# Handing over PSUM banks and halves one by one in a four-stage recurrent and attention network, with clock-keeping products in the last attention unit

## The chip, the cores and the metric

The kernel runs on one core of a Trainium2 chip. The metric is device time in microseconds (us) for one execution, from inputs in device memory to the output in device memory; lower is better. The engines are named as in the profile: PE is TensorE's matmul stream, PEld its weight loads, DVE is VectorE, ACT is ScalarE, POOL is GpSimd, SP issues DMAs. PSUM is the memory that TensorE writes; here it is used as eight banks of 512 float32 columns on 128 partitions.

## The reference

Sixteen sequences of 128 tokens with 256 channels pass through four layers, all in float32:

- a recurrent layer: layer norm, token shift (difference to the token before), five low-rank mixings of the shifted input, then projections of the mixed inputs to decay, key, value, receptance and gate; a recurrence `s = w * s + k v` with a state of 8 x 8 for each of 32 heads, read out by `r`; a norm over each head, the gate, an output projection and a residual; then a channel mix (layer norm, shift, `sigmoid(r) * (relu(k)^2 @ Wv)`) and a residual
- cross-attention to a context of 128 tokens with 16 heads of 16 channels, whose output goes through a projection and a scalar gate
- a second recurrent layer with other weights
- cross-attention with biases, followed by a layer norm and an MLP of 1024 hidden channels with GELU.

## The kernel before

The sequences are worked on in four groups of four (`G` = 4, `NB` = 4, `T` = 128 tokens, `C` = 256 channels in `HALF` = 2 halves of 128). Each group meets two mixers (one for each recurrent layer) and two attention units, so there are eight of each, in the order of `STEPS`. Three generator programs are interleaved on each engine:

- `head` (letter H): the first half of a mixer. Layer norm into `z`, transposed by TensorE into `PA`, copied to `XN`; `SX` is the shift; `mix` makes the first mixed input in `X5`; a low-rank product gives `low` and `thT`. Then for f = 0 to 4: `maa(f)` multiplies into both banks of `PA` (L990), `mix_low_rank` turns it into a mixed input in two passes over the two halves (L400, then L408), and a projection follows from `X5` into `PA` (L1022 and L1028 for the decay, L1046 for key, value and receptance, L1061 for the gate). `turn` (L417) transposes `PA` into the layout of the recurrence.
- `recurrence` (R): outer products `A_` (L425), scans (L498), products with `R_` (L506), and the sum over the state on TensorE (L1073), then norm, gate, output projection into `PB` (L1093) and the addition to `X`.
- `attn` (A): the channel mix (L576, L389, L954, L967, L586, L587), then the attention in 16 jobs of four heads each, its output projection (L967), and in layer 1 the MLP (L1255, L1264).

On every engine the strings of `ORDER` say which program advances to its next `yield`; each engine executes in that order and nothing overtakes. Engines meet through semaphores that are counted: `COUNTS` says how often each is raised in a unit. Before the change nearly all of them are raised once for a whole two-bank tile:

```python
for h in range(HALF):
    last = v.tensor_tensor(blocks(X5[use % 2][:])[:, h], split(pa4(h)), split(XN[:, h, :, 1:T + 1]), ALU.add)
last.then_inc(sem["r_mixed"], 1)
```

`keep_clock(o, n)` (L975) issues n products of the identity with itself that nobody reads; in `head` it is called through `fill`, for the first mixer only. A float32 product of 256 or 512 columns appears in the trace as two matmul records.

## Time and profile before

| | |
|---|---|
| Time, median of three runs | 1308.97 us (1307.58 to 1309.52) |
| The profiled execution | 1307.29 us, of which the trace's span is 1305.5 us |
| PE busy | 1127.7 us, 86% of the span |
| DVE busy | 859.1 us, 66% |
| ACT busy | 490.2 us, 38% |
| Mean granted TensorE clock | 0.923 of 2.4 GHz |

An engine's busy time is the sum of its instructions. A granted clock of 1.00 in a stretch means 2.4 GHz throughout, 0.50 means 1.2 GHz throughout. The chain that ended last is 63% PE and 26% DVE.

### The profile page before, as it was taken

What the parts mean: (1) busy time and instruction counts of PE and PEld (TensorE: products, weight loads), DVE (VectorE), ACT (ScalarE), POOL (GpSimd) and SP (SyncE); (2) the same over time, 40 slices, a digit from 0 to 9 for tenths busy, and PEclk for the clock granted to TensorE, in tenths of its full rate; (3) what the DMA queues carried; (4) which work ended last, traced back from release to release, by engine and by line L of the source; (5) the groups of instructions that cost most, each with busy time, mean ns of one, the idle gap of its engine ahead of it and who ended that gap; (6) DMA issues with size and microseconds to landing.
All of it is one profiled execution on the core that took longest, in us unless ns stands there. A gap on an engine that the chain in (4) does not pass through costs nothing.

```text
span 1305.5 us, 13985 instructions
## 1 busy us (share of the span) xinstructions
PE 1127.7 (86%) x5302; PEld 754.2 (58%) x5302; DVE 859.1 (66%) x1060; ACT 490.2 (38%) x1502; POOL 115.5 (9%) x92
## 2 busy tenths in 40 slices
PE   6856889898998898889798989989899898987868
PEld 4634557565756575647555756546656476564645
DVE  4597599769985997599755695446965459642320
ACT  1002215722572267215732732425332355221731
POOL 1021010101010100021000111000010001100000
PEclk9987889988998899979998989979999899997869
DMA  9000000000000000000000000000000000000000
GB/s 371 22 0 1 0 17 13 1 1 17 13 1 2 16 13 1 1 16 13 2 17 9 5 1 1 33 8 5 1 1 33 6 7 1 0 17 2 12 1 17
DMA packets 13317, 22.63 MB, mean 17 GB/s; under 512 B 3777, under 2 KB 10561, under 8 KB 12610
## 3 DMA queue, kind: packets, MB, share of 16 engines
...
## 4 chain that ended last, share of the span: by engine, by line
PE 63%; DVE 26%; ACT 5%; issue 4%; POOL 1%; DMA 1%; SPq 0%; POOLq 0%; DVEq 0%; ACTq 0%
PE QA L967 7%; PE PA L1046 6%; PE PB L1073 5%; DVE S_ L498 5%; PE QA L1264 4%; PE PA L990 4%; PE QB L1183 3%; PE QA L1159 3%; DVE A L506 3%; PE QB L954 2%; ACT big L889 2%; PE QA L1199 2%; DVE A L425 2%; PE QB L1112 2%; PE QB L1186 2%
## 5 line engine op out<-in xcount | busy, mean ns | idle before, releaser
L889 ACT ACTIVATE big<-QB,nmax 128x128 f32<-128x128 f32 x512 | 181.2, 375 | 72.8 <-DVE nmax L614 72.6
L498 DVE TENSOR_TENSOR_SCAN S_<-W_,A 128x1024 f32<-128x1024 f32 x64 | 154.3, 2432 | 0.2
L1073 PE MATMUL PB<-A,common_w 128*128 128x256 f32 x512 | 133.1, 405 | 23.0 <-DVE A L506 22.9
L614 DVE TENSOR_REDUCE nmax<-QB 128x4 f32<-128x512 f32 x128 | 86.7, 684 | 68.4 <-PE QB L1183 41.0
L1073 PEld LDWEIGHTS PB<-A,common_w 128*128 128x128 f32 x512 | 99.9, 204 | 49.9 <-DVE A L506 28.8
L1046 PE MATMUL PA<-rwkv_w,X 128*128 128x256 f32 x384 | 105.3, 426 | 11.6 <-DVE X L408 11.5
L889 ACT ACTIVATION_READ_ACCUMULATOR big<-QB,nmax 128x1 f32 x512 | 110.3, 215 | 0.0
L1183 PE MATMUL QB<-big,QX 128*128 128x256 f32 x384 | 101.2, 387 | 0.0
L1199 PE MATMUL QA<-common_w,big 128*128 128x128 f32 x512 | 83.1, 287 | 19.7 <-ACT XT L898 12.6
L1046 PEld LDWEIGHTS PA<-rwkv_w,X 128*128 128x128 f32 x384 | 79.2, 213 | 32.1 <-DVE X L408 17.2
L1199 PEld LDWEIGHTS QA<-common_w,big 128*128 128x128 f32 x512 | 63.0, 146 | 47.6 <-ACT big L889 22.0
L1183 PEld LDWEIGHTS QB<-big,QX 128*128 128x128 f32 x384 | 75.2, 196 | 13.3 <-issue 2.3
L400 DVE SCALAR_TENSOR_TENSOR PA<-PA,rwkv_w,SX 128x512 f32<-128x512 f32 x80 | 56.6, 752 | 39.9 <-PE PA L990 39.7
L990 PE MATMUL PA<-low,rwkv_w 32*128 32x512 f32 x128 | 64.0, 619 | 13.7 <-DVE K_ L417 8.5
L700 POOL TENSOR_SCALAR aveps<-amv 128x4 f32<-128x4 f32 x20 | 11.6, 578 | 707.8 <-DVE amv L373 707.8
L506 DVE TENSOR_TENSOR A<-R_,S_ 128x2048 f32<-128x2048 f32 x32 | 73.1, 2284 | 0.6
L425 DVE TENSOR_TENSOR A<-K_,V_ 128x2032 f32<-128x2032 f32 x32 | 72.6, 2267 | 1.3 <-PE PB L1073 0.7
L1177 PE MATMUL QB<-mrow,first_row 128*128 128x512 bf16 x128 | 50.4, 394 | 16.9 <-ACT big L889 16.0
L1264 PE MATMUL QA<-mlp_w,big 128*128 128x256 f32 x256 | 59.2, 384 | 0.8 <-ACT big L933 0.8
L898 ACT ACTIVATE XT<-QA 128x512 f32<-128x512 f32 x64 | 38.7, 605 | 40.1 <-PE QA L1199 40.0
L1264 PEld LDWEIGHTS QA<-mlp_w,big 128*128 128x128 f32 x256 | 47.6, 190 | 10.2 <-ACT big L933 1.6
L408 DVE TENSOR_TENSOR X<-PA,XN 128x512 f32<-128x512 f32 x80 | 51.4, 684 | 1.2
...
## 6 DMA issues: line engine op xcount, KB each, us to landing
rwkv_w<-in_rwkv_w SPq DMA_DIRECT2D x2, 2674.0 KB, 13.6
...
```

The source lines that it names most:

```text
L425: return v.tensor_tensor(A_[c % 2][:, :, :, 1:T], K_[:, :, 0:T - 1].unsqueeze(1).broadcast_to([P, DC, RS, T - 1]), V_[:, DC * c:DC * c + D ...
L498: last = v.tensor_tensor_scan(S_[:, d].rearrange("p k t -> p (k t)"), W_[:].rearrange("p k t -> p (k t)"), A_[c % 2][:, d].rearrange("p k ...
L506: v.tensor_tensor(A_[c % 2][:], R_[:].unsqueeze(1).broadcast_to([P, DC, RS, T]), S_[:], ALU.mult)\
L614: v.tensor_reduce(nmax[:, n % 2], bank(2 + n % 2).rearrange("p (j s) -> p j s", j=JH), AX.X, ALU.max, negate=True).then_inc(sem["a_max"], 1)
L889: last = s.activation(PR[:, n % 2, j], bank(2 + n % 2)[:, j * T:(j + 1) * T], ACT.Exp, bias=nmax[:, n % 2, j:j + 1], accum_out=den[:, b, h ...
L967: last = t.matmul(o, lhs(h, b), w[:, h], start=(h == 0), stop=(h == HALF - 1 and bias is None))
L990: last = t.matmul(pa(h), w2, tt, start=True, stop=True, tile_position=(rows, 0))
L1046: last = t.matmul(PA[:, a * C:(a + 1) * C], src[:, h, a * P:(a + 1) * P], wt[:, h], start=(h == 0), stop=(h == HALF - 1))
L1073: last = t.matmul(y, ident, A_[c % 2][:, :, k], start=(c % 2 == 0 and k == 0), stop=False, skip_group_check=True)
L1183: last = t.matmul(o, QX[b % 2][:, i, h], K2[:, :, h, b * T:(b + 1) * T], start=False, stop=True, skip_group_check=True)
L1199: last = t.transpose(bank(0)[:, j * T:(j + 1) * T], PR[:, n % 2, j], ident)
L1264: t.matmul(o, H_[:, m, b * T:(b + 1) * T], proj[:, m], start=(m == 0), stop=False)
```

## The change

- Hand-overs in halves. Nearly every semaphore that was raised once for a tile of two banks (or two halves) is raised once for each, and the consumer waits for the half that it needs. `mix`, `mix_low_rank` and `maa` signal each half; the subtraction of the token shift (`shift`) is issued for each half; `turn` is two transposes, one for each bank of `PA`, with a `yield` between; the additions to `X`, the square and centring in the norm of the recurrence, `tanh`, `relu` and square in ScalarE, the final addition and the store are in two parts.
- TensorE's token projections go by pairs: for two output blocks of 256 columns in one bank, first the products of channel half 0, then those of half 1 (`token_pair`). Number and size of the products stay the same.
- In the recurrence, the product that adds `V_` to `PB` goes before the last chunk rather than after it. The squares `SQ` are stored so that their sum reads neighbouring elements. `z` lives in `X5[0]` and not in `SX`.
- The first half of attention's output projection waits for `a_rb` and the first `a_on` only.
- Clock-keeping products: fewer in the first mixer (57 instead of 83), and new ones in the last attention unit (16, 2, 24, 3, 24 and 4 of them, 73 in all), written to `PA`.
- All four strings of `ORDER` are new. In VectorE's, the two outer products of the first mixer's recurrence (`RR`) now stand together right behind the turn of `V_`, with the mixing of f = 3 behind both; before, the mixing stood between them.

```diff
     "VectorE":
-        "HHAHHHHHHHHHHHRHHRHHHRRRRHRRRHRRRRHRRRRHHRRRHRHRRRHHHRAHAHHAAHRRHHAAHAHHRRRARARRRAAHRARARARARARAAHRR"
...
+        "HHAHHHHHHHHHHHHHHRRHHHHHHRRRRHRRRHRRHRRHRHRRRHHRRHRHRRRHHRHRRAHAHHAAHHRRHHAAAHHAHRRARARHRRARARRRAARH"
...
-        z = SX[:].rearrange("p h b t -> p (h b t)").rearrange("p (b c) -> p b c", b=NB)
         X5 = [sb(f"X5_{i}", [HALF, NB, T]) for i in range(2)]
+        z = X5[0][:].rearrange("p h b t -> p (h b t)").rearrange("p (b c) -> p b c", b=NB)
...
-        SQ = A_[1][:, 0]
+        SQ = A_[1][:, 0].rearrange("p k t -> p (k t)").rearrange("p (t d) -> p t d", d=RS)
...
-                        sp.wait_ge(sem["a_out"], u.at("a_out", 1))
-                        sp.dma_start(out[u.group], result).then_inc(sem["st_out"], 16)
-                sp.wait_ge(sem["st_out"], 16 * G)
+                        for k in range(2):
+                            sp.wait_ge(sem["a_out"], u.at("a_out", k + 1))
+                            sp.dma_start(out[u.group][:, 2 * k:2 * k + 2], result[:, 2 * k:2 * k + 2]).then_inc(sem["st_out"], 16)
+                sp.wait_ge(sem["st_out"], 32 * G)
...
                     for h in range(HALF):
-                        last = v.scalar_tensor_tensor(dst[:, h], sx[:, h], vec[:, h:h + 1], xn[:, h, :, 1:T + 1],
-                                                      ALU.mult, ALU.add)
-                    last.then_inc(done, 1)
+                        v.scalar_tensor_tensor(dst[:, h], sx[:, h], vec[:, h:h + 1], xn[:, h, :, 1:T + 1],
+                                               ALU.mult, ALU.add).then_inc(done, 1)
+
+                def shift(u, sx, xn, done):
+
+                    for h in range(HALF):
+                        dve.wait_ge(sem[done], u.at(done, h + 1))
+                        last = v.tensor_tensor(sx[:, h], xn[:, h, :, 0:T], xn[:, h, :, 1:T + 1], ALU.subtract)
+                    link(last)
 
...
                     for h in range(HALF):
-                        last = v.tensor_tensor(blocks(X5[use % 2][:])[:, h], split(pa4(h)), split(XN[:, h, :, 1:T + 1]), ALU.add)
-                    last.then_inc(sem["r_mixed"], 1)
+                        v.tensor_tensor(blocks(X5[use % 2][:])[:, h], split(pa4(h)), split(XN[:, h, :, 1:T + 1]), ALU.add)\
+                            .then_inc(sem["r_mixed"], 1)
 
                 def turn(u, n, dst):
 
-                    if n == 0:
-                        dve.wait_ge(sem["r_decay"], u.at("r_decay", 1))
-                    else:
-                        dve.wait_ge(sem["r_used"], u.at("r_used", n + 2))
-                    v.transpose(dst.rearrange("p k (a t) -> p a k t", a=TB),
-                                PA[:].rearrange("p (a k h) -> p a k h", a=TB, h=32))\
-                        .then_inc(sem["r_turned"], 1)
+                    to = dst.rearrange("p k (a t) -> p a k t", a=TB)
+                    of = PA[:].rearrange("p (a k h) -> p a k h", a=TB, h=32)
+                    for k in range(2):
+                        if n == 0:
+                            dve.wait_ge(sem["r_decay"], u.at("r_decay", k + 1))
+                        else:
+                            dve.wait_ge(sem["r_proj"], u.at("r_proj", 2 * (n - 1) + k + 1))
+                        if k:
+                            yield
+                        two = slice(TB // 2 * k, TB // 2 * (k + 1))
+                        v.transpose(to[:, two], of[:, two]).then_inc(sem["r_turned"], 1)
 
                 def outer(u, c):
 
...
                     yield
-                    v.scalar_tensor_tensor(YT[:], small[:, 0].unsqueeze(1).broadcast_to([P, RS, T]), -1.0 / RS, y,
-                                           ALU.mult, ALU.add).then_inc(sem["r_yc"], 1)
-                    yield
-                    dve.wait_ge(sem["r_sq"], u.at("r_sq", 1))
-                    v.tensor_reduce(small[:, 1], SQ.rearrange("p d t -> p t d"), AX.X, ALU.add).then_inc(sem["r_var"], 1)
+                    for k in range(2):
+                        v.scalar_tensor_tensor(YT[:, RS // 2 * k:RS // 2 * (k + 1)], small[:, 0].unsqueeze(1).broadcast_to([P, RS // 2, T]), -1.0 / RS,
+                                               y[:, RS // 2 * k:RS // 2 * (k + 1)], ALU.mult, ALU.add).then_inc(sem["r_yc"], 1)
+                    yield
+                    dve.wait_ge(sem["r_sq"], u.at("r_sq", 2))
+                    v.tensor_reduce(small[:, 1], SQ, AX.X, ALU.add).then_inc(sem["r_var"], 1)
...
-                    v.scalar_tensor_tensor(xf, PB[:], 0.5, xf, ALU.mult, ALU.add).then_inc(lane_sem["x_done"][u.lane], 1)
+                    for h in range(HALF):
+                        dve.wait_ge(sem["r_yn"], u.at("r_yn", h + 1))
+                        v.tensor_tensor(YG[:, h].rearrange("p b (a t) -> p a b t", a=TB),
+                                        GN[:, h].rearrange("p (a b t) -> p a b t", a=TB, b=NB),
+                                        blocks(Gt[u.index % 2][:])[:, h], ALU.mult).then_inc(sem["r_yg"], 1)
+                    for k in range(2):
+                        yield
+                        dve.wait_ge(sem["r_o"], u.at("r_o", k + 1))
+                        part = slice(512 * k, 512 * k + 512)
+                        last = v.scalar_tensor_tensor(xf[:, part], PB[:, part], 0.5, xf[:, part], ALU.mult, ALU.add)
+                    last.then_inc(lane_sem["x_done"][u.lane], 1)
...
-                    link(v.scalar_tensor_tensor(cf, CR, 1.0, QB[:], ALU.add, ALU.mult))
...
+                            yield
+                        part = slice(512 * k, 512 * k + 512)
+                        dve.wait_ge(sem["f_rr"], u.at("f_rr", k + 1))
+                        dve.wait_ge(sem["f_v"], u.at("f_v", k + 1))
+                        link(v.scalar_tensor_tensor(cf[:, part], CR[:, part], 1.0, QB[:, part], ALU.add, ALU.mult))
+                        last = v.scalar_tensor_tensor(xf[:, part], cf[:, part], 0.5, xf[:, part], ALU.mult, ALU.add)
+                    last.then_inc(lane_sem["x_done"][u.lane], 1)
 
                     yield
                     if not mlp:
...
+                def chan_proj(dst, w, src, done, ready):
 
                     for m in range(HALF):
                         for h in range(HALF):
+                            if m == 0:
+                                ready(h)
                             last = t.matmul(dst[:, m * 512:(m + 1) * 512], w[:, h, m * P:(m + 1) * P], src[:, h],
                                             start=(h == 0), stop=(h == HALF - 1))
-                    last.then_inc(done, 1)
...
+                def token_pair(dst, w, lhs, k, ready, bias=None):
+
+                    for h in range(HALF):
+                        ready(h)
+                        for b in (2 * k, 2 * k + 1):
+                            last = t.matmul(dst[:, b * C:(b + 1) * C], lhs(h, b), w[:, h], start=(h == 0 and b == 2 * k),
+                                            stop=(h == HALF - 1 and bias is None), skip_group_check=True)
+                    if bias is not None:
+                        for b in (2 * k, 2 * k + 1):
+                            last = add_bias(dst[:, b * C:(b + 1) * C], bias, True)
+                    return last
+
+                def token_proj(dst, w, lhs, done, ready, bias=None):
+
+                    for k in range(2):
+                        if k:
+                            yield
+                        token_pair(dst, w, lhs, k, ready if k == 0 else lambda h: None, bias).then_inc(done, 1)
...
+                            ready(h)
                             rows = MIX * f % P if f < 4 else P - MIX
                             w2 = r_(L, "w2a" if f < 4 else "w2b")[rows:rows + MIX, h * P:(h + 1) * P]
                             tt = (low if f < 4 else thT)[rows:rows + MIX]
-                            last = t.matmul(pa(h), w2, tt, start=True, stop=True, tile_position=(rows, 0))
-                        last.then_inc(sem["r_maa"], 1)
+                            t.matmul(pa(h), w2, tt, start=True, stop=True, tile_position=(rows, 0)).then_inc(sem["r_maa"], 1)
...
                     last.then_inc(sem["r_used"], 1)
+                    fill(4)
+                    yield
+                    maa(0, lambda h: pe.wait_ge(sem["r_lowrank"], u.at("r_lowrank", h + 1)))
                     fill(6)
                     yield
...
                     for f, w in ((1, "Wk"), (2, "Wv"), (3, "Wr")):
                         yield
-                        pe.wait_ge(sem["r_turned"], u.at("r_turned", f))
-                        maa(f)
-                        fill(9)
-                        yield
-                        pe.wait_ge(sem["r_mixed"], u.at("r_mixed", f + 2))
+                        maa(f, turned(f - 1))
+                        fill(6)
+                        yield
                         src = flat(X5[(f + 1) % 2])
                         wt = rh_(L, w)
-                        for a in range(TB):
-                            if a:
+                        for k in range(2):
+                            if k:
                                 yield
                             for h in range(HALF):
-                                last = t.matmul(PA[:, a * C:(a + 1) * C], src[:, h, a * P:(a + 1) * P], wt[:, h],
-                                                start=(h == 0), stop=(h == HALF - 1))
-                        last.then_inc(sem["r_used"], 1)
-                        if f < 3:
-                            fill(4)
-                    yield
-                    pe.wait_ge(sem["r_turned"], u.at("r_turned", 4))
-                    maa(4)
-                    yield
-                    pe.wait_ge(sem["r_mixed"], u.at("r_mixed", 6))
+                                if k == 0:
+                                    mixed(f + 1)(h)
+                                for a in (2 * k, 2 * k + 1):
+                                    last = t.matmul(PA[:, a * C:(a + 1) * C], src[:, h, a * P:(a + 1) * P], wt[:, h],
+                                                    start=(h == 0 and a == 2 * k), stop=(h == HALF - 1), skip_group_check=True)
+                            last.then_inc(sem["r_proj"], 1)
+                    yield
+                    maa(4, turned(3))
+                    yield
                     wg = rh_(L, "Wg")
                     for m in range(HALF):
                         if m:
                             yield
                         for h in range(HALF):
+                            if m == 0:
+                                mixed(5)(h)
                             last = t.matmul(pa(m), wg[:, h, m * P:(m + 1) * P], flat(X5[1])[:, h], start=(h == 0), stop=(h == 1))
-                    last.then_inc(sem["r_used"], 1)
+                        last.then_inc(sem["r_wg"], 1)
...
+                        if c == NCH - 1:
+                            yield
+                            pe.wait_ge(sem["r_vr"], u.at("r_vr", 1))
+                            for h in range(HALF):
+                                t.matmul(pb(h), ident, V_[:, h * RS // 2:(h + 1) * RS // 2], start=False, stop=False,
+                                         skip_group_check=True)
...
-                    pe.wait_ge(sem["r_vr"], u.at("r_vr", 1))
-                    for h in range(HALF):
-                        if h:
-                            yield
-                        last = t.matmul(pb(h), ident, V_[:, h * RS // 2:(h + 1) * RS // 2], start=False, stop=True,
-                                        skip_group_check=True)
-                    last.then_inc(sem["r_y"], 1)
...
+
+                    def fill(n):
+                        if u.index == len(ATTENTIONS) - 1:
+                            keep_clock(PA[:, 0:P], n)
...
+                    if u.index == len(ATTENTIONS) - 1:
+                        pe.wait_ge(sem["r_gate"], MIXERS[-1].at("r_gate", 1))
                     pe.wait_ge(sem["f_z"], u.at("f_z", 1))
                     turn_tokens(bank, az, sem["f_zT"])
...
+                    fill(16)
+                    yield
+                    chan_proj(QB, rh_(L, "fWk"), C5[0].rearrange("p h b t -> p h (b t)"), sem["f_k"],
+                              lambda h: pe.wait_ge(sem["f_mixed"], u.at("f_mixed", h + 1)))
+                    fill(2)
+                    yield
+                    yield from token_proj(QA, rh_(L, "fWr"), lambda h, b: C5[1][:, h, b], sem["f_r"],
+                                          lambda h: pe.wait_ge(sem["f_mixed"], u.at("f_mixed", h + 3)))
+                    yield
+                    yield from token_proj(QB, rh_(L, "fWv"), lambda h, b: CK[:, h, b], sem["f_v"],
+                                          lambda h: pe.wait_ge(sem["f_kk"], u.at("f_kk", h + 1)))
+                    fill(24)
...
+                    fill(3)
+                    chan_proj(QA, ah_(L, "Wq"), XT, sem["a_qp"], lambda h: pe.wait_ge(sem["a_xc"], u.at("a_xc", h + 1)))
...
+                    pe.wait_ge(sem["a_rb"], u.at("a_rb", 2))
+                    pe.wait_ge(sem["a_on"], u.at("a_on", 1))
+                    token_pair(QA, ah_(L, "Wo"), lambda h, b: CT[:, h, b * T:(b + 1) * T], 0, lambda h: None,
+                               1 if mlp else None).then_inc(sem["a_o"], 1)
+                    yield
                     pe.wait_ge(sem["a_on"], u.at("a_on", 2))
-                    token_proj(QA, ah_(L, "Wo"), lambda h, b: CT[:, h, b * T:(b + 1) * T], sem["a_o"],
-                               1 if mlp else None)
+                    token_pair(QA, ah_(L, "Wo"), lambda h, b: CT[:, h, b * T:(b + 1) * T], 1, lambda h: None,
+                               1 if mlp else None).then_inc(sem["a_o"], 1)
                     if mlp:
+                        fill(24)
                         yield
                         pe.wait_ge(sem["a_z"], u.at("a_z", 2))
                         turn_tokens(lambda h: bank(2 + h), az, sem["a_xT"])
+                        fill(4)
```

## Rows read from the trace of the kernel before

**Rows 1.** The page: the span, and busy time of TensorE and VectorE.
```profile
span 1305.5 us, 13985 instructions
...
PE 1127.7 (86%) x5302; PEld 754.2 (58%) x5302; DVE 859.1 (66%) x1060; ACT 490.2 (38%) x1502; POOL 115.5 (9%) x92
```

**Rows 2.** Windows: busy time (instructions) by engine, granted clock, DMA share, GB/s.
```profile
0.00:105.50 105.50, 75.20 (x318) 52.49 (x319) 67.12 (x78) 8.41 (x13) 17.11 (x19) 0.90 0.32 122
75.00:100.00 25.00, 13.45 (x40) 8.94 (x39) 24.73 (x24) 1.46 (x3) 5.12 (x2) 0.84 0.00 0
105.50:1170.00 1064.50, 951.23 (x4513) 636.47 (x4511) 762.11 (x927) 432.82 (x1322) 95.95 (x70) 0.94 0.03 8
1170.00:1305.50 135.50, 101.28 (x472) 65.29 (x472) 29.90 (x56) 48.98 (x168) 2.40 (x4) 0.81 0.03 7
```

**Rows 3.** Waits of PE in 105.5 to 1170: total, times, longest us.
```profile
PE QB L947 <- DVE az L378: 14.9, 7, 3.3
PE PA L1022 <- DVE X L408: 13.6, 6, 5.4
...
PE PA L1046 <- DVE X L408: 9.3, 8, 1.8
PE PA L990 <- DVE K_ L417: 8.0, 5, 2.4
PE PA L990 <- DVE R_ L417: 7.8, 4, 2.1
PE PA L1007 <- DVE X L389: 5.9, 2, 2.9
PE PA L990 <- ACT thT L767: 3.8, 3, 1.3
```

**Rows 4.** Timeline, 36 to 47: start, length, instructions, [idle before <- releaser].
```profile
36.86 1.98 PE L990 MATMUL PA<-low,rwkv_w 32*128 32x512 f32 x4 [0.45 <-DVE Gt L417]
...
38.77 2.27 PE L975 MATMUL PB<-common_w 128*128 128x128 f32 x18
38.88 1.42 DVE L400 SCALAR_TENSOR_TENSOR PA<-PA,rwkv_w,SX 128x512 f32<-128x512 f32 x2 [2.07 <-PE PA L990]
40.33 1.29 DVE L408 TENSOR_TENSOR X<-PA,XN 128x512 f32<-128x512 f32 x2
...
41.67 3.72 PE L1046 MATMUL PA<-rwkv_w,X 128*128 128x256 f32 x16 [0.63 <-DVE X L408]
...
45.43 1.25 DVE L417 STREAM_TRANSPOSE K_<-PA 128x1024 f32<-128x1024 f32 x1 [3.81 <-PE PA L1046]
```

**Rows 5.** Groups by line, VectorE: busy us, mean ns, then idle before.
```profile
L425 DVE TENSOR_TENSOR A<-K_,V_ 128x2032 f32<-128x2032 f32 x32 | 72.6, 2267 | 1.3 <-PE PB L1073 0.7
...
L527 DVE TENSOR_REDUCE small<-A 128x128 f32<-128x1024 f32 x8 | 15.3, 1917 | 8.6 <-ACT A L795 8.6
...
L540 DVE TENSOR_TENSOR S_<-S_,Gt 128x512 f32<-128x512 f32 x16 | 10.3, 688 | 10.9 <-ACT S_ L802 10.9
...
L445 DVE TENSOR_TENSOR SX<-XN 128x1024 f32<-128x1024 f32 x8 | 9.8, 1223 | 5.9 <-ACT XN L746 5.8
```

**Rows 6.** Timeline of the last attention unit, PE, 1170 to 1305.5.
```profile
1175.09 6.24 PE L954 MATMUL QB<-XT,rwkv_w 128*128 128x512 f32 x8 [3.81 <-DVE XT L389]
...
1195.74 1.97 PE L947 MATMUL QA<-common_w,az 128*128 128x128 f32 x8 [7.50 <-DVE az L378]
1198.58 6.44 PE L1159 MATMUL QA<-XT,attn_w 128*128 128x512 f32 x8 [0.87 <-ACT XT L820]
...
1266.60 1.97 PE L947 MATMUL QB<-common_w,az 128*128 128x128 f32 x8 [5.96 <-DVE az L378]
1269.43 5.16 PE L1255 MATMUL QA<-XT,mlp_w 128*128 128x512 f32 x8 [0.87 <-ACT XT L820]
1274.43 3.60 PE L1255 MATMUL QB<-XT,mlp_w 128*128 128x512 f32 x8
```

**Rows 7.** Timeline of the final addition, VectorE.
```profile
1301.22 1.22 DVE L667 TENSOR_TENSOR XT<-QA,X 128x1024 f32<-128x1024 f32 x1 [34.68 <-PE QA L960]
```

227 lines of the change are left out of this document (103 added, 124 removed).

## The prediction

> **What bounds the kernel now.** I read the page first, then windows, then waits, and the timeline where single durations mattered. The page gives a span of 1305.5 us with PE busy for 1127.7 of it and DVE for 859.1 [rows 1]. PE is the nearest thing to a bound, but two things keep the span above its work: 178 us in which it is idle, and stretches at half its clock.
>
> The windows cut the span in three [rows 2]. To 105.5 us, when the second group's head begins, PE is busy 75.2 us: one head runs alone, a chain from engine to engine, and then the recurrence follows, in which DVE is busy 24.73 of 25 us. From 105.5 to 1170 head, recurrence and attention overlap: 951.2 of 1064.5 us busy, 113 idle, clock 0.94. From 1170 on the last attention unit is alone: 101.3 of 135.5 busy, clock 0.81. A lost clock share costs time only where PE works: (1 - 0.94) x 1064.5 = 64 us, times the busy share 0.89, is 57 us in the middle; (1 - 0.81) x 135.5 x 0.75 = 19 us at the end.
>
> For the middle the waits of PE say which hand-over ended the idle time [rows 3]. The reader is to see two kinds. Waits for mixed inputs (L1022, L1046, L1007: 13.6 + 9.3 + 5.9 = 28.8 us) and for the turned tile or the low-rank `tanh` (L990: 8.0 + 7.8 + 3.8 = 19.6 us) are on hand-overs that the change halves, 48.4 us together. The 14.9 us for `az` are not: the layer norm, with its POOL step, stays whole. The rest (scans, softmax) is not touched either.
>
> **The change, part by part.**
>
> *One step of the head.* Rows 4 hold one f. Before: `maa` 1.98 us, L400 starts when both banks are there and takes 1.42, L408 1.29, sixteen records of L1046 until the turn can start at 45.43, the turn 1.25, next `maa` at 46.7. The period is 9.9 us. After, with half durations of 0.71, 0.65, 0.65 and about 0.1 from engine to engine: `maa` half 0 is out at 1.1, half 1 at 2.1; L400 runs 1.1 to 1.8 and 2.1 to 2.8; L408 2.85 to 3.5 and 3.5 to 4.15; the first pair of L1046 can start at 3.55 and ends at 5.3, the second at 7.0; the first turn is over at 6.0, so the next `maa` starts at 7.0, while the second turn (7.1 to 7.7) hides behind its half 0. The period becomes 7.0, a gain of 2.9 us for each f. The same overlay gives 0.6 for the shift, 0.7 for the first mix, 0.6 for the low-rank `tanh`, 1.4 for f = 0 and 1.4 for the decay.
>
> *The first 105.5 us.* Up to the turn of R these add to 4.7 + 3 x 2.9 - about 1 (the last turn has nobody behind it) = 12.4 us. The fewer fills, six of about 0.22 us (eighteen records, two for each, took 2.27 with the modelled end of the last [rows 4]), fit the shorter gap. Against it stands the new order: both outer products, 2.27 us each [rows 5], precede L400 of f = 3; before, they lay in its waits. L400 then waits about 4.3 us, and R's turn, POOL's products and the scans behind it too. I take 12.4 - 4.3 = 8 us, with 3 and 13 as ends. DVE sets the pace afterwards, and nothing is gained there.
>
> *The middle.* In the step above the gap ahead of L1046 falls from 2.8 us to 1.55, some 45%, and the one ahead of `maa` goes. Applied to rows 3: 0.45 x 28.8 + 0.95 x 19.6 = 32 us. That is 28% of the 113 idle us; if the clock's loss falls in proportion, 0.28 x 57 = 16. Together 48. The half additions and the product with `V_` moved ahead shorten tails by 1 to 2 us a group, but these run beside other groups' work, and I count nothing.
>
> *What it costs.* The split puts two instructions in the place of one on DVE eleven or twelve times for each group and layer (shift, four turns, centring, addition in the mixer; shift, two steps of the channel mix, one or two additions in attention). One such split costs 2 x 0.688 - 1.223 = 0.15 us [rows 5]. Seven groups' worth in the middle, about 82 splits, is 12 us; the contiguous sum gives back up to 0.7 of L527's 1.917, seven times, 5 us. No row has a two-bank transpose halved or ScalarE writing `SQ` with a stride; I take the same 0.15 for the one and nothing for the other, since ACT waits more than it works there (38% busy). Net 7 us, of which DVE's busy share (762 of 1064) lies in the way: 5 us. The Trainium skill's page Perfetto Trace Analysis (Optimizing Scalar/DVE Operations) speaks on both sides: breaking up instructions helps engines that cause bubbles, grouping helps a saturated one, and the overhead it states is about 60 ns in SBUF and 125 ns in PSUM; by that, 82 splits would cost an estimated 5 to 10 us rather than 12. The trace has both cases, bubbles in the head and a saturated DVE in the scans.
>
> So 43 us for the middle by rows 3. But gaps that close bring forward what queues next: the 14.9 us for `az`, the scans' and softmax's waits, none of them shortened. A quarter of the gain I give back to these, and take 32, between 0 (all goes to the next wait) and 60 (the tails count too).
>
> *The last unit*, alone on the engines, so that each term is on the path [rows 6]. The shift and mix halves make L954's input ready 1.3 us earlier; but sixteen fills of 0.22 us fill the gap and end 0.5 us before the old start: 0.5. L954 took 6.24 us at half clock where the same shape takes 3.60 (row of 1274.43): 2.6. Two fills ahead of L967: -0.4. The channel mix's two additions follow the first half: 1.1. The transposes of 1195.74 to the start of L1159 took 2.84; at full clock, with Wq on the first half and behind three fills, 1.7: 1.1. L1159 6.44 against 3.60: 2.8. The first softmax jobs ran at half clock too and should gain between 0 and 4: 2.5. Attention's output projection starts before the last product (0.7) and its addition is halved (0.5): 1.2; its clock I leave, as no fill stands ahead of it. Transposes and fills before L1255: 0.9. L1255 5.16 against 3.60: 1.5. The last addition, 1.22 us [rows 7], and the store go in halves: 0.6. Sum 14.4 us, ends 8 and 20: at the low end the 24 fills run at half clock and delay the transposes behind them, at the high end the clock holds in the output projection too.
>
> **Sum.** 8 + 32 + 14.4 = 54 us from 1307.3 us, the profiled execution's own time, is 1253; it lies 1.7 us below the median of the runs, so the forecast for the median is 1254 us, 4.2% less.
>
> **The rivals.**
>
> *Next wait takes over (the middle gains nothing).* For it: three fifths of the middle's idle time is on waits that stay, and DVE is saturated beside the scans. Against it: PE's idle time directly ahead of L990 and L1046 is on the longest chain of the head, and no other engine is near its limit there. Then 8 + 14 = 22 us: 1287 us.
>
> *The whole overlay counts.* Head and tails shorten everywhere and the new order uses it: 12 + 60 + 18 = 90 us: 1219 us. For it: PE's own work, 1128 us less the half-clock loss, leaves that room. Against it: nothing outside the head and the end is shortened.
>
> *Slower.* One mechanism: in a pair, successive products write different columns of a bank and come back to the first. If the alternation broke the overlap of weight load and product, it would hit the token projections of all units, L1046, L967 and L1093: by the code eight tiles in each group and layer, 64 in all, of 16 records each, so 1024 records, which now follow each other at about 0.22 us (16 in 3.72 us [rows 4]). It decides against the gain at 0.05 us a record; at a quarter more, 0.055, the time is 1254 + 56 = 1310, and at 0.10 us it is 1354. Against it: weights change from product to product before as well, and the columns change too.
>
> *The clock-keeping does not do what it says* (the clock stays low at the end, or fills delay): part of the last unit's low end, 6 us, 1260; inside the range.
>
> **How the numbers follow.** My forecast, with the fills' failure in it, 1232 to 1275: 0.62. Next wait takes over, 1275 to 1300: 0.18. Whole overlay, below 1232: 0.13. Slower: 0.05; the remaining 0.02 is no change. The range for 8 in 10 reaches to 1222 and 1291, into both neighbours. The limit between same and changed is 0.2%, 2.6 us, about what runs of this kernel differ by. Faster: 0.62 + 0.18 + 0.13 = 0.93; same 0.02; slower 0.05.
>
> **What the profile of the changed kernel would show.** Span near 1251; PE idle in all near 145 us with PE busy near 1105; mean clock near 0.95. In the first head the starts of successive L990 groups 7 to 8 us apart, with some 4 us of delay ahead of the mixing of f = 3, and the first scan near 65 instead of 73.3. L1159 and L954 in the last unit at 3.6 us, window clock there above 0.9. PE's waits for X at L1046 and L1022 cut by about half and those for the turned tiles near nothing; those for `az` unchanged or longer. Records of pairs still 0.22 us apart. It would make me wrong if PE's waits moved to DVE's scans in the middle, if ordered work stood in line ahead of the head's short steps (the `RR` pattern in every group), or if fills stood between data and a waiting product.

## The result and the profile after

The changed kernel takes 1274.45 us (median of 4 runs, 1272.81 to 1275.06) against 1309.24 us before on the same chip: a ratio of 0.9735, with a 95% interval of 0.9718 to 0.9751. It is 34.8 us faster. The forecast was 1254 us; the range of 1222 to 1291 holds the result, but the likeliest value is 20 us too low. What follows is mostly about those 20 us.

The page answers to [rows 1]: span 33 us shorter, TensorE (PE) busy almost as long as before although it is idle 30 us less.

```profile
span 1272.4 us, 14341 instructions
...
PE 1124.9 (88%) x5396; PEld 760.6 (60%) x5396; DVE 859.5 (68%) x1152; ACT 501.7 (39%) x1542; POOL 106.6 (8%) x92
```

The windows are cut at two events: the transposes of the second head, as in [rows 2], and the end of the last mixer's addition to `X`, from which on the last unit runs alone. (In the kernel before this end lies at 1165.3 us, 4.7 us ahead of the cut in [rows 2].) In the columns stand the busy time and instructions of PE, PEld, DVE, ACT and POOL, then the granted clock, the DMA share and GB/s.

```profile
0.00:93.60 93.60, 68.58 (x251) 44.61 (x251) 59.08 (x79) 8.59 (x14) 14.32 (x18) 0.85 0.35 137
93.60:1143.20 1049.60, 944.23 (x4523) 635.10 (x4524) 766.49 (x1000) 443.17 (x1356) 88.68 (x68) 0.95 0.03 8
1143.20:1272.40 129.20, 112.06 (x625) 80.89 (x623) 33.95 (x75) 49.95 (x172) 3.60 (x6) 0.91 0.03 8
```

The middle still has 105 us of idle PE, against 112 before between the same two events. Its waits, which answer to [rows 3] (total, times, longest):

```profile
PE QB L981 <- DVE az L378: 26.7, 7, 5.7
PE QB L1221 <- ACT big L923: 22.2, 23, 3.4
PE PA L1097 <- DVE X L416: 12.4, 7, 3.8
PE PB L1128 <- DVE A L517: 6.2, 5, 2.6
PE PA L1058 <- DVE X L389: 5.2, 2, 3.7
...
PE QA L1243 <- ACT XT L932: 4.7, 3, 2.5
...
PE PA L1036 <- DVE K_ L431: 2.8, 1, 2.8
...
PE QA L1243 <- ACT az L947: 2.3, 3, 0.8
PE PA L1036 <- DVE R_ L431: 2.3, 3, 1.2
...
PE QA L1243 <- ACT CN L932: 2.2, 3, 1.2
...
PE PA L1072 <- DVE X L416: 1.2, 2, 0.6
```

The short steps of the head did what the sum said: the waits for the turned `K_` and `R_` (L1036, before L990) have gone from 15.8 to 5.1 us, L1072 (before L1022) from 13.6 to 1.2. But the wait for `az`, which isn't halved, grew from 14.9 to 26.7 us, and the projections of the head (L1097, before L1046) wait longer than before, 12.4 against 9.3. The wait for the softmax's exponentials (L1221, before L1177) grew as well, from 12.3 to 22.2; but the softmax's other wait (L1243, before L1199, 16.6 us in three rows) fell to 9.2, so that the softmax as a whole waits only 2.5 us more.

One step f of the first head, to be read against [rows 4]:

```profile
34.51 1.98 PE L1036 MATMUL PA<-low,rwkv_w 32*128 32x512 f32 x4
...
35.66 1.62 DVE L406 SCALAR_TENSOR_TENSOR PA<-PA,rwkv_w,SX 128x512 f32<-128x512 f32 x2 [0.35 <-PE PA L1036]
...
37.32 1.29 DVE L416 TENSOR_TENSOR X<-PA,XN 128x512 f32<-128x512 f32 x2
...
38.07 3.72 PE L1097 MATMUL PA<-rwkv_w,X 128*128 128x256 f32 x16
40.10 0.72 DVE L431 STREAM_TRANSPOSE K_<-PA 128x512 f32<-128x512 f32 x1 [1.49 <-PE PA L1097]
41.72 2.00 PE L1036 MATMUL PA<-low,rwkv_w 32*128 32x512 f32 x4
41.83 0.72 DVE L431 STREAM_TRANSPOSE K_<-PA 128x512 f32<-128x512 f32 x1 [1.01 <-PE PA L1097]
```

These lines show the hand-overs in halves: L1097 starts 0.75 us after L416 has begun its first half, the second half of the turn starts together with the next L1036, and the period is 41.72 - 34.51 = 7.2 us (9.9 before; 7.0 predicted). Sixteen records of a pair still take 3.72 us, as before, so alternating between the columns of a bank costs nothing that shows here.

In the last unit, to be read against [rows 6]:

```profile
1149.79 4.37 PE L1020 MATMUL PA<-common_w 128*128 128x128 f32 x32
1154.00 3.60 PE L990 MATMUL QB<-XT,rwkv_w 128*128 128x512 f32 x8
...
1171.39 1.10 PE L981 MATMUL QA<-common_w,az 128*128 128x128 f32 x8 [1.08 <-DVE az L378]
...
1172.99 3.63 PE L990 MATMUL QA<-XT,attn_w 128*128 128x512 f32 x8
...
1239.03 3.60 PE L1306 MATMUL QA<-XT,mlp_w 128*128 128x512 f32 x8
```

All three projections run at the full 2.4 GHz: 3.60 us where 6.24, 6.44 and 5.16 stood. The unit takes 129.2 us from the last addition to `X` to the end, against 140.2 before (1165.3 to 1305.5): 11.0 us less.

### The profile page after: what moved, and what is told of

Its sections match the earlier page's. It is cut to its first block, busy times and chain, and to the rows that moved or that the text cites. A ratio compares the mean times of both kernels' runs of the same rounds, so it can differ in the third digit from the quotient of the medians.

```text
span 1272.4 us, 14341 instructions
## 1 busy us (share of the span) xinstructions
PE 1124.9 (88%) x5396; PEld 760.6 (60%) x5396; DVE 859.5 (68%) x1152; ACT 501.7 (39%) x1542; POOL 106.6 (8%) x92
## 4 chain that ended last, share of the span: by engine, by line
PE 63%; DVE 24%; ACT 5%; issue 4%; POOL 3%; DMA 1%; SPq 0%; DVEq 0%; POOLq 0%; ACTq 0%
PE PA L1097 7%; PE QA L1003 6%; DVE S_ L509 5%; PE PB L1128 5%; PE QA L1315 5%; PE QB L990 4%; PE QB L1227 3%; PE PA L1036 3%; ACT big L923 3%; DVE az L378 3%; PE QA L1243 3%; DVE A L517 2%; PE QA L990 2%; DVE A L437 2%; PE QA L1306 2%
## 5 line engine op out<-in xcount | busy, mean ns | idle before, releaser
L923 ACT ACTIVATE big<-QB,nmax 128x128 f32<-128x128 f32 x512 | 181.4, 378 | 88.2 <-DVE nmax L632 88.1
L509 DVE TENSOR_TENSOR_SCAN S_<-W_,A 128x1024 f32<-128x1024 f32 x64 | 149.0, 2349 | 0.2
L1128 PEld LDWEIGHTS PB<-A,common_w 128*128 128x128 f32 x512 | 98.3, 201 | 34.6 <-DVE A L517 15.1
L1097 PE MATMUL PA<-rwkv_w,X 128*128 128x256 f32 x384 | 100.8, 416 | 16.8 <-DVE X L416 16.6
L923 ACT ACTIVATION_READ_ACCUMULATOR big<-QB,nmax 128x1 f32 x512 | 111.8, 218 | 0.0
L1097 PEld LDWEIGHTS PA<-rwkv_w,X 128*128 128x128 f32 x384 | 78.1, 209 | 34.3 <-DVE X L416 21.6
L1243 PE MATMUL QA<-common_w,big 128*128 128x128 f32 x512 | 83.8, 289 | 12.5 <-ACT XT L932 5.9
L1243 PEld LDWEIGHTS QA<-common_w,big 128*128 128x128 f32 x512 | 63.1, 147 | 40.5 <-issue 24.3
L1221 PE MATMUL QB<-mrow,first_row 128*128 128x512 bf16 x128 | 51.3, 401 | 26.4 <-ACT big L923 25.4
L1036 PE MATMUL PA<-low,rwkv_w 32*128 32x512 f32 x128 | 66.4, 636 | 4.3 <-DVE K_ L431 2.8
L416 DVE TENSOR_TENSOR X<-PA,XN 128x512 f32<-128x512 f32 x80 | 51.5, 685 | 1.3
## 6 DMA issues: line engine op xcount, KB each, us to landing
rwkv_w<-in_rwkv_w SPq DMA_DIRECT2D x2, 2674.0 KB, 14.4
```

The source lines that it names most:

```text
L509: last = v.tensor_tensor_scan(S_[:, d].rearrange("p k t -> p (k t)"), W_[:].rearrange("p k t -> p (k t)"), A_[c % 2][:, d].rearrange("p k ...
L923: last = s.activation(PR[:, n % 2, j], bank(2 + n % 2)[:, j * T:(j + 1) * T], ACT.Exp, bias=nmax[:, n % 2, j:j + 1], accum_out=den[:, b, h ...
L1036: t.matmul(pa(h), w2, tt, start=True, stop=True, tile_position=(rows, 0)).then_inc(sem["r_maa"], 1)
L1097: last = t.matmul(PA[:, a * C:(a + 1) * C], src[:, h, a * P:(a + 1) * P], wt[:, h], start=(h == 0 and a == 2 * k), stop=(h == HALF - 1), s ...
L1128: last = t.matmul(y, ident, A_[c % 2][:, :, k], start=(c % 2 == 0 and k == 0), stop=False, skip_group_check=True)
L1243: last = t.transpose(bank(0)[:, j * T:(j + 1) * T], PR[:, n % 2, j], ident)
```

## The experiments

Besides medians I use milestones: the start of the first exponential of an attention unit (the first record of the group that is L923 after the change), and the end of the span. All in us, from the profiled executions. Each ratio is to the kernel before, timed beside the run on the same chip; the medians of before differ by up to 2 us from chip to chip, so small differences between runs of different chips are read from the ratios.

```
                    unit 1  unit 5  unit 6  unit 8     end
before               205.2   711.9   874.3  1208.1  1305.5
after                190.8   689.9   860.0  1179.7  1272.4
outer                184.8   684.0   854.1  1173.8  1266.5
old_order            186.9   681.5   835.1  1156.0  1248.7
old_whole_head       202.7   704.4   861.8  1187.0  1279.8
new_then_old         196.9   730.4   884.6  1205.0  1294.9
old_then_new         187.8   689.0   872.9  1219.2  1312.6
old_then_new_fine    186.9   687.0   861.4  1187.0  1279.8
```

### The three parts of the change: products, halves, order

Four kernels take the change apart. **fill_only** is the kernel before with the 73 clock-keeping products of the last unit alone:

```diff
+                    def fill(n):
+                        if u.index == len(ATTENTIONS) - 1:
+                            keep_clock(PA[:, 0:P], n)
...
                     turn_tokens(bank, az, sem["f_zT"])
+                    fill(16)
```

> The kernel before, with only the 73 clock-keeping products of the last attention unit added at the same places. If they work by the clock (theory 1): L954 and L1159 of the last unit near 3.6 us instead of 6.2 and 6.4, L1255 near 3.6 instead of 5.2, less about 1 us of delay by the products themselves, so 6 us less than before, near 1303. If they mostly delay what waits behind them (theory 2): 1308 or more.

Measured: 1300.70 us, ratio 0.9940 [0.9924, 0.9957], 8.3 us less, as theory 1 has it: L954 takes 3.70 us there, the first projection of the MLP 3.70 and L1169 (L1159 before) 3.98. **no_fill** is the changed kernel without them:

```diff
                     def fill(n):
-                        if u.index == len(ATTENTIONS) - 1:
-                            keep_clock(PA[:, 0:P], n)
+                        return
```

> The changed kernel without the 73 products of the last unit; nothing else differs. Theory 1 (they give the clock back): L990 and L1306 of the last unit return to 5 to 6.5 us, and the time rises by 6 to 8 us, to 1281 or 1282. Theory 2 (shorter gaps keep the clock by themselves): within 2 us of the changed kernel.

Measured: 1279.69 us, 0.9771 [0.9755, 0.9787]; by the ratios the products are worth 0.0036, or 4.7 us, in the changed kernel. Without them L990 takes 6.46 and 5.81 us and L1305 (L1306 after the change) 5.75, so theory 1 holds, with a gain a little below its 6 to 8 us. They work in both kernels; whether they are worth less beside the halves (4.7 against 8 us) is within the intervals.

**old_order** keeps all halves, pairs and products, and goes back to the issue order of before: the `ORDER` strings of before, and the `yield`s where they were, so that one letter means as much work as before.

```diff
 ORDER = {
     "VectorE":
-        "HHAHHHHHHHHHHHHHHRRHHHHHHRRRRHRRRHRRHRRHRHRRRHHRRHRHRRRHHRHRRAHAHHAAHHRRHHAAAHHAHRRARARHRRARARRRAARH"
+        "HHAHHHHHHHHHHHRHHRHHHRRRRHRRRHRRRRHRRRRHHRRRHRHRRRHHHRAHAHHAAHRRHHAAHAHHRRRARARRRAAHRARARARARARAAHRR"
...
                     for k in range(2):
...
-                        if k:
-                            yield
                         two = slice(TB // 2 * k, TB // 2 * (k + 1))
```

> All half hand-overs, pairs and the last unit's products of the changed kernel, but with the four order strings of the kernel before (instructions that got a step of their own go with their neighbour). Theory A (the halves gain where a group is alone, the next wait takes over elsewhere, the order matters little): 15 to 30 us less than before, 1280 to 1294. Theory B (the new order throws away what the halves gave): 1255 to 1268. Theory C (the gain of the change is mostly the new order's): 1295 or more.

Measured: 1250.62 us, 0.9559 [0.9545, 0.9573]: 58.4 us faster than before and 24 us faster than the change. That is below every range expected, and nearest to theory B: the new order gives back part of what the halves gained. Its windows, cut at the same events:

```profile
0.00:97.20 97.20, 70.21 (x267) 48.01 (x268) 68.44 (x83) 8.59 (x14) 17.12 (x19) 0.86 0.34 132
97.20:1121.00 1023.80, 933.25 (x4498) 629.48 (x4497) 762.40 (x997) 443.02 (x1354) 94.78 (x68) 0.95 0.03 9
1121.00:1248.70 127.70, 112.83 (x635) 81.03 (x633) 33.90 (x74) 50.49 (x174) 3.60 (x6) 0.92 0.03 8
```

The middle is 26 us shorter than after the change, the last unit nearly the same. The halves and products are worth 58 us; the new order takes 24 of them back. In the waits of the middle:

```profile
PE QB L974 <- DVE az L379: 18.9, 7, 3.9
...
PE QB L1222 <- ACT big L916: 12.5, 19, 1.6
...
PE PA L1063 <- DVE X L417: 7.9, 3, 3.8
PE PA L1088 <- DVE X L417: 5.7, 6, 1.0
...
PE PA L1049 <- DVE X L390: 2.6, 2, 1.3
```

PE is idle for 90.6 us of this middle, 14.8 less than in the changed kernel; the waits for `az` (18.9 against 26.7) and of the head's projections (L1088, 5.7 against 12.4) differ by 14.5 together. In the whole span the two kernels differ by 23.7 us, of which 15.1 are idle time of PE and 8.6 busy time.

**whole_head** is the changed kernel in which the heads wait for whole tiles again:

```diff
-                        dve.wait_ge(sem["r_maa"], u.at("r_maa", 2 * f + h + 1))
+                        dve.wait_ge(sem["r_maa"], u.at("r_maa", 2 * f + 2))
...
-                        return lambda h: pe.wait_ge(sem["r_mixed"], u.at("r_mixed", 2 * use + h + 1))
+                        return lambda h: pe.wait_ge(sem["r_mixed"], u.at("r_mixed", 2 * use + 2))
```

> The changed kernel, but TensorE waits for both halves of the mixed input, of the turned tile and of the low-rank tanh, and VectorE for both halves of maa's product; all instructions and signals stay. Theory A (the head's halves are on the path only while few groups are in flight, in the first two heads): some 12 us for the first head, 6 for the second, 1 to 2 for each other, 25 to 30 us in all, 1300 to 1305. Theory D (they are on the path in all eight heads): 8 x 10 us, 1350. Theory E (hidden nearly everywhere): below 1285.

Measured: 1315.03 us, 1.0047 [1.0032, 1.0062]: 40.6 us slower than the change and slower than the kernel before. No theory's range holds: the waits are worth more than the 25 to 30 us of theory A, half of theory D's 80. **old_whole_head** is the same edit in the old order:

> The halves with the order of before (1250.6 us), but in the heads TensorE waits for both halves of each mixed input, turned tile and low-rank product, and VectorE for both banks of the low-rank product, as before the change. With nothing in halves and the clock-keeping products kept, the kernel took 1300.7 us, so that all halves together are worth 50 us in this order. Theory A, the heads' halves are most of it, about 4 to 5 us in each of 8 heads as the prediction's overlay has it: 1280 to 1291. Rival: in an order made for whole banks the heads' halves are worth less than 20 us and the tails' and attention's pairs the rest: 1260 to 1270.

Measured: 1280.76 us, 0.9796 [0.9776, 0.9815], 30 us above old_order. Theory A holds at its lower edge. From fill_only (0.9940) to old_order (0.9559) all halves together are worth 50 us, with the pairs and the smaller changes that come along (the earlier product with `V_`, the layout of `SQ`, the place of `z`, the fewer products in the first mixer): 30 of them lie in the waits of the heads, 20 in everything else. The same waits are worth 41 us in the new order, which leans on them more.

### Where the order loses

**outer** undoes one exchange in the first group of the new order: VectorE's second outer product goes behind the mixing for f = 3 again, as before the change; the first stays ahead of it.

```diff
-        "HHAHHHHHHHHHHHHHHRRHHHHHHRRRRHRRR...
+        "HHAHHHHHHHHHHHHHHRHHRHHHHRRRRHRRR...
```

> The changed kernel with one edit of its order: in the first group VectorE issues the first outer product before, and not after, the mixing for f = 3. The prediction said that the two outer products placed ahead of that mixing cost 4.3 us in the first group, and that the rest of the order costs nothing. If that is so, the first scan comes near 66 instead of 70.1 us; how much of it reaches the end is open: 1270 to 1274 us. Rival: the price of the order isn't in this place; with one product (2.3 us) still ahead of the mixing, the first scan stays within 1 us of 70.1 and the end at 1274.

Measured: 1269.25 us, 0.9712 [0.9696, 0.9728]: 5.2 us less by the medians, 3.0 by the ratios, whose intervals still touch. (The first sentence expected of this run has the products the wrong way round: the first one stood ahead of the mixing all along, as the rival says.) The first scan starts at 63.7 us, and the time lies just below the 1270 to 1274 of the theory, so this place does cost time. Between the two profiled executions the span falls by 5.9 us, and every milestone by 5.9 or 6.0. The timeline of the changed kernel at this place:

```profile
49.80 4.59 DVE L437 TENSOR_TENSOR A<-K_,V_ 128x2032 f32<-128x2032 f32 x2
...
54.43 1.42 DVE L406 SCALAR_TENSOR_TENSOR PA<-PA,rwkv_w,SX 128x512 f32<-128x512 f32 x2
...
56.63 6.49 PE L1097 MATMUL PA<-rwkv_w,X 128*128 128x256 f32 x16 [4.14 <-DVE X L416]
```

And of outer:

```profile
48.45 2.27 DVE L437 TENSOR_TENSOR A<-K_,V_ 128x2032 f32<-128x2032 f32 x1
...
50.76 1.42 DVE L406 SCALAR_TENSOR_TENSOR PA<-PA,rwkv_w,SX 128x512 f32<-128x512 f32 x2
...
52.95 3.72 PE L1097 MATMUL PA<-rwkv_w,X 128*128 128x256 f32 x16 [1.83 <-DVE X L416]
```

With two products ahead, PE waits 4.14 us for its input and then works at half clock, 6.49 us instead of 3.72; with one, it waits 1.83 and keeps the clock. (The granted clock from the start of these products to their end is 0.57 in the changed kernel and 1.00 in outer.) So one exchange costs 2.3 us of waiting and 2.8 of clock, 5.1 together. 1.4 us more lie ahead of this place, where the code is the same and the two executions differ already; they aren't an effect of the edit. Of the 6.4 us at the first scan (70.1 against 63.7) 5.9 reach the end in this pair, and 3 to 5 us by the medians of all runs.

An early delay is not always kept like this. old_sq and tail_fill, below, have the old order and the same instructions up to the last units. In the profiled executions the first scan of old_sq starts 2.7 us later (66.3 against 63.6), and at the first exponential of unit 2 both stand at 311.9 us. There the old order took up the whole delay within two units.

The next question was whether the other 18 us (20 by the ratios) lie at one place. **new_then_old** and **old_then_new** change orders at the end of the fourth attention unit; both keep the coarse steps of before, so that the new order is rounded to them.

```diff
     "VectorE":
...
-        "HRARAARHARARARRAARHARARARAAAHHAARRAARARRRHHARARAAHAAHHAAHAHHAAAAHRAARAHAAHAAAAAAHAHARARARARARRRAHRRA"
+        "HRARAARHARARARRAARHARARARAAAHHAARRAARARRRHHARRAAAAAHAAHHAHAAHHAAHAAARARAHHAAAHAAAHRRAARRARARARARRARA"
```

These are the letters of old_then_new at its seam; on each engine the steps that are still open there follow in the other order's sequence.

> The halves with the new order up to the end of the fourth attention unit, and from there the order of before. Theory P: the 8 to 12 us lost by then stay lost, 1259 to 1263. Theory Q: they are made up later, 1250 to 1254. Third: the new order's second half is what loses, and the first only moves work about: then this one is near 1250 and the kernel with the new order second near 1274.

> The halves with the order of before up to the end of the fourth attention unit (near 620 us), and from there the new order with its steps cut as in the kernel before. The new order's loss was 24 us at the end, 8 to 12 of them by the softmax of the fourth and fifth attention unit and some 16 between those of the fifth and the sixth. Theory P, the loss is made in each stretch by what the order does there: this one ends 12 to 16 us above 1250.6, at 1262 to 1267. Theory Q, the new order lives on a lead that it builds early and its second half is no worse: 1250 to 1255.

Measured: 1296.59 us, 0.9910 [0.9881, 0.9938], and 1315.49 us, 1.0063 [1.0044, 1.0081]. No expectation held. The milestones say more than the ends. From the first exponential of unit 5 to the end the old order takes 564.5 us behind the new one and 567.2 behind itself: here it matters little what went before. The new order takes 582.5 us in the changed kernel, and 623.6 when rounded to coarse steps. Rounding costs its first half too: 730.4 against 689.9. So I ran **old_then_new_fine**, in which both parts have exactly the instruction sequences of old_order and of the changed kernel. Behind the seam its letters are those of the change:

```diff
     "VectorE":
...
-        "HAAAHHAHHAAHHRRHHAAAHHAHHRARRRARRRAAHHRAARARARARARARRAAHAARARAHHARARRARARARARAARAAHHAAHHAAAHHAHHAAHHAA"
+        "ARRAHHAHHAAHHRAAHHARHHAHHRRARARHRARAARHARARARRAARHARARARAAAHHAARRAARARRRHHARARARAAAAHHAAAHHAHHAAHHAA"
         "HAAHARARAHHAAAHAHAAHRRAARRARARARARRARARARARRRHRRHHRHARRRARRRAHHAAAHHAAAHHAHHHHAAHHAAHHARAHHARAHAHAHA"
```

> As old_then_new (order of before up to the end of the fourth attention unit, then the new order), but with the second part issued in exactly the changed kernel's own small steps and not in the coarser steps of before. With coarse steps the second part took 624 us from the first exponential of the fifth attention unit to the end, against 582.5 in the changed kernel and 567 in the order of before. Theory P (the new order loses locally, and it needs its small steps): the second part takes 580 to 586 here too, and the kernel 1264 to 1270. Rival (the seam between two orders is what cost, whatever the steps): above 1290.

Measured: 1281.83 us, 0.9805 [0.9787, 0.9822]. The second part takes 592.8 us: 31 us less than in coarse steps, 26 more than in the old order, 10 more than in the changed kernel. Of these 10, what the seam costs and what the new order costs I can't separate. The kernel lies between the two ranges expected (1264 to 1270, and above 1290). That the order loses where it is used fits the 26 us, but the seam's share in them isn't shown. The changed kernel and old_order show the largest loss between the first exponentials of units 5 and 6, 170.1 us against 153.6. The windows of that stretch, after the change and in old_order:

```profile
689.90:860.00 170.10, 150.08 (x698) 98.96 (x697) 107.66 (x148) 66.26 (x197) 13.97 (x11) 0.96 0.03 9
```

```profile
681.50:835.10 153.60, 141.66 (x666) 93.05 (x665) 102.51 (x142) 66.17 (x197) 17.05 (x11) 0.95 0.03 10
```

The new order runs 32 more matmul records in this stretch, 28 of them head projections (L1097) and 4 `maa` products (L1036), which keep PE busy 8.4 us longer; and PE is idle 8.1 us longer (20.0 against 11.9). It pulls work of the next head ahead of the attention unit in hand, and by the end nothing has come back: 24.9 us behind at the first exponential of unit 6, 23.7 at the end.

### The term counted at nothing: the square written with a stride

**old_sq** is old_order with the square's layout of before.

```diff
-        SQ = A_[1][:, 0].rearrange("p k t -> p (k t)").rearrange("p (t d) -> p t d", d=RS)
+        SQ = A_[1][:, 0]
```

> The kernel with the halves but the order of before (1250.6 us), and the square laid out as before: ScalarE writes it contiguously (halves near 0.57 us instead of 1.16), VectorE sums it with a stride (1.92 instead of 1.21 us). On the path of a tail that is 1.2 less and 0.7 more, 0.5 us in each of 8 tails. Theory: the strided write that the prediction counted at nothing costs these 0.5 us where the tail is on the path: 1246.5 to 1250. Rival: the tails lie beside other work in all units but the last: 1250 to 1251.

Measured: 1245.73 us, 0.9527 [0.9513, 0.9541]; by the ratios 4.2 us less than old_order, by the spans 4.7, a little more than the theory's best. The square in old_order, where it is written with a stride, and the sum in the changed kernel, which reads neighbouring elements (in old_order the mean sum is 1220 ns):

```profile
L817 ACT ACTIVATE A<-YT 128x512 f32<-128x512 f32 x16 | 16.4, 1131 | 15.1 <-DVE YT L534 15.1
...
L539 DVE TENSOR_REDUCE small<-A 128x128 f32<-128x1024 f32 x8 | 9.7, 1213 | 5.2 <-ACT A L824 5.0
```

The same two in old_sq:

```profile
L817 ACT ACTIVATE A<-YT 128x512 f32<-128x512 f32 x16 | 9.4, 626 | 16.4 <-DVE YT L534 16.4
...
L538 DVE TENSOR_REDUCE small<-A 128x128 f32<-128x1024 f32 x8 | 15.3, 1917 | 7.5 <-ACT A L817 7.5
```

With a step of eight fp32 elements, 32 bytes, from one element to the next of its output, a half square costs 505 ns more (535 in the changed kernel, where its mean is 1161). The sum costs 697 ns less than with the old layout, where the eight elements that it adds up lie 128 elements, 512 bytes, apart. A tail has two squares and one sum: 1.01 us against 0.70, so 0.31 us in each of eight tails, 2.5 in all. The rest of the 4.2 us is within the intervals of the two ratios. The Trainium skill, in SBUF — State Buffer (Door 1: The DMA port swizzle), says that one can step over SBUF for free only within a 16-byte line, four fp32 elements. Both steps here are longer, and the trace agrees on both: 1131 against 626 ns for the write, 1917 against 1220 for the read. Each of the two layouts has such a step on one side, and the change chose the one for which a tail pays twice.

### A version that beats both

In old_sq the last tail's turned tile is ready at 1099.08 us and its transposes start at 1107.62, because two output products of the attention unit before stand ahead of them in PE's order (timeline of old_sq):

```profile
1097.83 1.25 DVE L545 STREAM_TRANSPOSE A<-A 128x1024 f32<-128x1024 f32 x1
1099.90 3.72 PE L1315 MATMUL QA<-mlp_w,big 128*128 128x256 f32 x16
1103.76 3.72 PE L1315 MATMUL QA<-mlp_w,big 128*128 128x256 f32 x16
1107.62 1.09 PE L974 MATMUL PB<-common_w,A 128*128 128x128 f32 x8
```

**tail_fill** starts from old_sq and rearranges this end.

```diff
     "TensorE":
...
-        "AAAAAARARAARRHARRRRHRRARRAAAAAARRARRARRAAAARARRRRAAAAAAAAAAAAAAAAAAAAAAAAAAAAAAAAAAAAAAAAAAAAAAAAAAA"
+        "AAAAAARARAARRHARRRRHRRARRAAAAAARRARRARRAARAARRRRAAAAAAAAAAAAAAAAAAAAAAAAAAAAAAAAAAAAAAAAAAAAAAAAAAAA"
...
                     turn_tokens(bank, az, sem["f_zT"])
-                    fill(16)
+                    if final:
+                        late_values(0)
+                        keep_clock(PB[:, 0:P], 6)
...
-                    fill(24)
+                    if final:
+                        chan_proj(PB, ah_(L, "Wk"), ctx_chan, sem["a_kp"], lambda h: None)
+                        late_values(1)
...
                             scores(n + 2)
+                            fill(1)
```

> The halves with the order of before and the contiguous square (1245.7 us), with the last stretch rearranged: the last tail's transposes go ahead of the last two output products of the attention unit before instead of behind them; the last unit's context keys and values are projected in the gaps where 40 of the clock-keeping products stood, into PA and PB; 20 clock-keeping products more stand before and in the softmax, 4 ahead of its last product. Theory: TensorE gets to the last unit's first turned tile 4 to 5 us sooner and its first scores 5 to 6 us sooner; if the added products keep the clock at 1.0 through the softmax and the Wo product, another 4 to 8 us: 1232 to 1241. Rival: the chain is ScalarE's and VectorE's there, or the added products delay the scores: 1241 to 1247.

Measured: 1240.20 us, 0.9486 [0.9467, 0.9505], in the theory's range. The turned tile came 4.0 us sooner (1117.23 instead of 1121.19), and then this happened:

```profile
1107.92 3.72 PE L1157 MATMUL PB<-rwkv_w,S_ 128*128 128x256 f32 x16
1117.23 1.94 PE L997 MATMUL QA<-common_w,az 128*128 128x128 f32 x8 [5.59 <-DVE az L379]
1118.97 3.51 PE L1019 MATMUL PA<-attn_w,ctx 128*128 128x256 f32 x8
```

With the keys gone from that gap PE stood idle for 5.59 us, the clock fell to 1.2 GHz, and the next products took 1.94 and 3.51 us. So the last unit's first exponential starts only 1.2 us sooner (1150.2 against 1151.3). The rest of the gain of 5.5 us lies behind it: old_sq runs at half clock from 1153.5 to 1163.7 and from 1191.0 to 1201.3, tail_fill only from 1190.5 to 1193.9. **tail_keys** puts the keys back there and 26 clock-keeping products into their place.

```diff
-                    if mlp and not final:
+                    if mlp:
                         yield from keys_values(ctx_chan)
...
-                        chan_proj(PB, ah_(L, "Wk"), ctx_chan, sem["a_kp"], lambda h: None)
                         late_values(1)
+                        fill(26)
```

> As tail_fill (1240.2 us), where TensorE stood idle for 5.6 us ahead of the last unit's first turned tile (1111.6 to 1117.2 us) and then ran at half clock until 1122.2. Here the context keys' projection (3.6 us) goes back into that gap, and 26 clock-keeping products stand in its later place. Theory: ScalarE scales the keys before the turned tile needs it, and with less idle time the clock stays at 1.0: the first f product starts at 1121 to 1122 instead of 1124.2, the end at 1236 to 1238.5. Rival: the clock falls all the same, or ScalarE is late: 1239 to 1242.

```profile
1111.38 3.60 PE L1002 MATMUL QB<-ctx,attn_w 128*128 128x512 f32 x8
1117.14 1.06 PE L993 MATMUL QA<-common_w,az 128*128 128x128 f32 x8 [2.16 <-DVE az L379]
1118.04 1.89 PE L1015 MATMUL PA<-attn_w,ctx 128*128 128x256 f32 x8
...
1121.62 3.60 PE L1002 MATMUL QB<-XT,rwkv_w 128*128 128x512 f32 x8
```

The place behaved as expected: idle 2.16 us, full clock, the first f product at 1121.62 instead of 1124.17. But the kernel takes 1241.63 us, 0.9485 [0.9472, 0.9498], the same as tail_fill, with the same span of 1238.5 us: behind the softmax a half-clock stretch that was 3.4 us long (1190.5 to 1193.9) is now 6.8 us (1187.0 to 1193.8), and the last exponential's lead of 1.2 us is gone by the output projection. The time is the rival's, but for neither of its two reasons: the clock held where the edit was, and ScalarE was in time. So 1240 us, 5.1% below before, is where these experiments end.

## Why the prediction was right or wrong

**One step of the head**, predicted 7.0 us, took 7.2. Its shape (next `maa` at the end of the second pair, second turn hidden) is as forecast.

**The result as a whole.** The forecast's own band was 1232 to 1275, and 1274.45 lies in it by half a microsecond. The halves and products without the new order take 1250.6, close to the likeliest value of 1254; what the new order adds, 24 us, is a loss for which the sum held 4.3. That it still ended inside the band is luck.

**The first group**, predicted 8 us less with the first scan near 65: it starts at 70.1 instead of 73.3, 3.2 us less; in old_order at 65.0 (63.5 to 66.3 in the four kernels that have this first group, in one profiled execution each). Of the overlay's 12.4 us old_order shows 8.3; the 4 us between may be outer products that lay in waits which are gone (L1097 still waits 1.83 us in outer), but no run takes them out. In the change the term that failed is the 4.3 us for both products. As a wait it was right (4.14 us), but the clock fell in that wait, which adds 2.8. And "DVE sets the pace afterwards, and nothing is gained there" missed that something can be lost there: from the first to the last scan of this group the new order takes 37.2 us, 70.1 to 107.3, the old one 31.5, 65.0 to 96.5, with steps of the second head ordered between the scans; that these are the cause was not tested alone. Most of it comes back at first: at the first exponential of unit 1 the new order is 3.9 us behind (190.8 against 186.9).

**The middle**, predicted 32 us less. Taking 3.2 us for the first scan and 11.0 for the last unit from the 33.1 us of the span leaves 18.9. In old_order the same sum is 56.8 - 8.3 - 12.5 = 36.0. So the working by rows 3, a quarter given back, was good for the halves, and its waits bear it out: those for mixed inputs fell in old_order from 28.8 to 16.2 us (7.9 + 5.7 + 2.6), by 44% where the sum had 45%. The step that failed is in the part on the change: I priced the new order by one pair of letters in the first group and took the rest at nothing, though all four strings of it are new. I had named it ("if ordered work stood in line ahead of the head's short steps") as what would make me wrong, and gave it no price.

**The costs.** A split costs 2 x 0.710 - 1.245 = 0.17 us on a two-bank transpose, 0.15 to 0.16 on additions, as taken. The 92 splits add 14.9 us of instruction time. DVE's busy time stayed at 859.5 us all the same, mostly because the sums took 5.6 us less, as forecast, and the 64 scans 5.4 us less, which no term of the sum held (2349 ns each instead of 2432; the last section has the reason). ScalarE's strided write, counted at nothing because ACT waits more than it works, costs 1.01 to 1.07 us a tail, against 0.70 that the sum gives back. The argument was wrong in kind: an engine that is mostly idle is still on the path where its one instruction is waited for.

**The last unit**, predicted 14.4 us less: 11.0. All projections came to 3.6 us as forecast. Up to the first exponential the terms add to 7.7 us, and 6.3 came (42.8 us before, 36.5 after); behind it they add to 6.7, and 4.7 came. Ahead of it, the 16 products take 4.37 us, part of them at half clock (granted clock 0.84): L990 starts at 1154.0 behind them, 1.7 us after the first half of its input was ready, where the sum had them end ahead of the input. What is missing behind it isn't traced to one place. The output projection, whose clock the sum had left as it was, takes 3.78 us for its first pair, at half clock, and 2.11 for its second.

**What I said the profile would show.** Idle time of PE 145 us: 147.5. Busy time 1105 us: 1124.9. The miss is in busy time, where I hadn't added the 73 products of about 0.23 us, 17 us. The clock gave back less than in the old order: PE's busy time at half clock went from 157 to 139 us, in old_order to 127.

**The rivals.** "Next wait takes over" describes part of it: `az` does wait longer, 14.9 us before, 18.9 in old_order and 26.7 after the change. The first 4.0 us came with the halves, the other 7.8 with the order. The softmax's two waits together stand at 28.9 us before, 32.4 in old_order and 31.4 after, so they take little. The slowdown by alternating columns didn't occur (its 1354 us should have read 1356: 1024 records at 0.10 us are 102 us). That the products would fail didn't either. That the whole overlay counts (1219 us) is borne out by no run: old_order, without the new order's loss, took 1250.6.

What stays open: which exchanges in the order cost the 18 us outside the first group. The strings of the four engines belong together, and only whole stretches were tried.
